# A four-layer model on one core: the pieces of work laid between the steps of an LSTM, cut finer and placed anew

## The reference, cut to what matters

```python
x = x + L0_conv(ln_c(x))   # two Mamba2 blocks along the 32 columns of a row; state and rows in sequence
t = x + L0_ffn(ln_t(x))    # 8 experts of two layers with batch norm, softmax over 8
x = t + L1_conv(ln_c(t))   # log-sum-exp product with an accumulator (V, H, 64, 64)
x = x + L1_ffn(ln_t(x))    # 8 experts, GELU, top 2
x = x + L2_conv(ln_c(x))   # a second log-sum-exp product
x = x + L2_ffn(ln_t(x))    # an LSTM over all 1024 tokens
x = x + L3_conv(ln_c(x))   # 7x7 depthwise convolution, then attention over 1024 tokens
x = x + L3_ffn(ln_t(x))    # 8 experts, top 2

def step(carry, xs):        # of the LSTM, 1024 of them, one after the other
    h, c = carry; xi, xf, xg, xo = xs
    i = sigmoid(xi + h @ V_i); g = tanh(xg + h @ V_c); o = sigmoid(xo + h @ V_o)
    c_new = h * c + i * g
    h_new = o * tanh(c_new)
```

## Time and profile before

| | |
|---|---|
| three runs, median (lowest to highest) | 3486.21 (3484.66 to 3487.12) us |
| the profiled execution, its own time | 3478.68 us |
| its span, first to last instruction | 3476.9 us |
| mean granted TensorE clock | 0.789 |
| first h of the LSTM, last h | 293.7 us, 2842.3 us |
| instructions in the span | 72552 |

### The profile page before, as it was taken

One profiled execution on the slowest core, in us unless ns is written; L12 is line 12 of the kernel. 1 busy time (PEld: TensorE's weight loads), 2 busy tenths in 40 slices (PEclk: granted clock), 3 DMA queues, 4 the chain that ended last, 5 costly groups with the idle time before them and its releaser, 6 DMA issues. The chain is left out here.

```text
span 3476.9 us, 72552 instructions
## 1 busy us (share of the span) xinstructions
PE 2849.0 (82%) x22302; PEld 2325.8 (67%) x22302; DVE 2121.4 (61%) x8884; ACT 1696.4 (49%) x5788; POOL 766.8 (22%) x1419
## 2 busy tenths in 40 slices
PE   4477888898888888889898888889888669887675
PEld 3365666677777777777777777777777554555565
DVE  4566566666666666666666666666644322556777
ACT  1254555555565565555555555555555322443232
POOL 2233222222222222222232222222211000000100
PEclk9687666688787888888888877877867669998677
DMA  2000000000010000000000000000000000000000
GB/s 92 12 16 16 16 17 17 17 18 19 19 31 18 18 18 18 18 18 17 18 17 18 19 19 23 26 18 17 17 16 8 3 16 11 1 1 3 8 7 8
DMA packets 53970, 59.73 MB, mean 17 GB/s; under 512 B 26448, under 2 KB 45008, under 8 KB 53200
## 3 DMA queue, kind: packets, MB, share of 16 engines
q1 hardware_dynamic: 53584, 54.98, 5.3%
HBM read 42.35 MB, written 4.19 MB: 13 GB/s over the span
## 5 line engine op out<-in xcount | busy, mean ns | idle before, releaser
L1116 DVE TENSOR_TENSOR_SCAN r_c<-r_wk 64x24 f32<-64x24 f32 x1024 | 272.6, 266 | 588.8 <-ACT r_wk L1102 576.9
L1091 PEld LDWEIGHTS psL<-r_h,lv 128*64 128x64 f32 x2048 | 244.7, 164 | 509.7 <-DVE r_h L1121 372.8
L1091 PE MATMUL psL<-r_h,lv 128*64 128x8 f32 x2048 | 324.3, 231 | 304.1 <-DVE r_h L1121 271.7
L1102 ACT ACTIVATE r_wk<-psL 64x16 f32<-64x16 f32 x1024 | 189.4, 185 | 688.2 <-PE psL L1092 674.0
L1196 PE MATMUL psL<-img,dg 128*128 (+1 forms) x2744 | 439.9, 318 | 1.1 <-DVE r_h L1121 1.1
L1196 PEld LDWEIGHTS psL<-img,dg 128*128 128x128 f32 x2744 | 399.0, 226 | 6.3 <-issue 1.2
L1107 ACT ACTIVATE r_tc<-r_c 64x8 f32<-64x8 f32 x1024 | 217.2, 212 | 277.0 <-DVE r_c L1116 223.6
L1093 PE MATMUL psL<-r_h,lv 128*64 128x8 f32 x2048 | 330.2, 234 | 0.0
L1092 PE MATMUL psL<-r_h,lv 128*64 128x8 f32 x2048 | 308.2, 223 | 0.0
L1121 DVE SCALAR_TENSOR_TENSOR r_h<-r_wk,r_tc 64x8 f32<-64x8 f32 x1024 | 187.3, 183 | 138.2 <-ACT r_tc L1107 128.9
L1092 PEld LDWEIGHTS psL<-r_h,lv 128*64 128x64 f32 x2048 | 257.7, 174 | 0.0
(11 more groups left out here) (407 smaller groups left out, 6709.0 us busy)
## 6 DMA issues: line engine op xcount, KB each, us to landing
accb<-acc_in SPq DMA_DIRECT2D x64, 512.0 KB, 3.5
a_xy<-a_E SPq DMA_DIRECT2D x512, 16.0 KB, 1.8
W<-pack_in SPq DMA_DIRECT2D x1, 3165.0 KB, 14.1
x6d<-X SPq DMA_DIRECT2D x64, 32.0 KB
out_x<-X SPq DMA_DIRECT2D x32, 64.0 KB, 1.6
X<-x_in SPq DMA_DIRECT2D x1, 1856.0 KB, 18.1
W<-pack_in SPq DMA_DIRECT2D x1, 1331.0 KB, 5.6
X<-x_in SPq DMA_DIRECT2D x1, 192.0 KB, 6.2
```

The lines of the kernel that those rows point to most:

```text
L1091: nc.tensor.matmul(psL[0:64, par, c:c + LB], lv[:, 0], h, start=False, stop=False, skip_group_check=True)
L1102: nc.scalar.activation(o, psL[0:64, par, c:c + 2 * LB].rearrange("p (g b) -> p g b", b=LB), ACT.Tanh).then_inc(sem("r_gi"), 1)
L1116: v.tensor_tensor_scan(r_c3[:, t % 2, :], r_wk[:, 0:24], r_wk[:, 30:54], 0.0, ALU.mult, ALU.add).then_inc(sem("r_c"), 1)
```

## The change

The generators of the parts yield more often, so that a piece is one or two instructions where it was two to eleven, and the rows of `TIMES` have more entries and other due times. `SAME` marks a yield that has no due time of its own where no table is used (in the last phase), so nothing changes there. The hardware loop is gone: all turns are written out by the same Python code. No instruction of the computation is added, removed or altered; only their order on each engine changes, and in the turns of the former loop the waits and addresses are constants in place of register arithmetic.

```diff
 TIMES = {
     mybir.EngineType.SP: (
-        (20.5,), (17.5,), (28,), (11,), (6,),
+        (17,), (13.5,), (28,), (9,), (7.5,),
...
     mybir.EngineType.Activation: (
...
-        (2, 5, 8, 8.5, 10, 13, 20, 25, 30),
+        (3, 3, 5, 5, 8, 8, 8, 9, 10.5, 13, 17.5, 27, 27, 30),
...
@@ mamba_pe
             for j in range(J):
                 if j:
                     yield
                 for h in range(NH):
+                    if h and h % 2 == 0:
+                        yield
                     last = nc.tensor.matmul(...)
@@ mamba_pool
             for j in range(J):
+                if j:
+                    yield
                 last = g.tensor_tensor(u["xw"][:, j], ...)
@@ ffn0_act
                     for q in (2 * n, 2 * n + 1):
+                        if q % 2:
+                            yield
                         last = nc.scalar.activation(f_h[:, q], ..., ACT.Relu, ...)
@@ mix_act
                 for e in (2 * n, 2 * n + 1):
+                    if e % 2:
+                        yield
                     last = nc.scalar.activation(u["h"][:, e], ..., ACT.Gelu, ...)
@@ conv_pe
-                for ky, kx in TAPS[n:n + count]:
+                for c, (ky, kx) in enumerate(TAPS[n:n + count]):
+                    if c and c % 2 == 0:
+                        yield
                     last = nc.tensor.matmul(o, dg[:, ky * KT + kx], rows[...], ...)
@@ weave
                     while due <= slot:
-                        due = next(g, None)
+                        new = next(g, None)
+                        due = due if new == SAME else new
@@ turns
-            with eng.Fori(FIRST_FULL, LAST_FULL, 2) as i:
-                turn(i, FIRST_FULL % 2)
-                turn(i + 1, (FIRST_FULL + 1) % 2)
-            for i in range(LAST_FULL + 1, NT + 1):
+            for i in range(FIRST_FULL, NT + 1):
                 turn(i, i % 2)
```

More of the change, by code:

```diff
@@ L79 @@
     mybir.EngineType.SP: (
-        (20.5,),
-        (17.5,),
+        (17,),
+        (13.5,),
         (28,),
-        (11,),
-        (6,),
+        (9,),
+        (7.5,),
     ),
     mybir.EngineType.Pool: (
-        (29.5, 29.5, 31, 31),
-        (30,),
-        (9.5,),
+        (23.5, 26, 26, 27),
+        (24,),
+        (15,),
         (0,),
-        (10.5,),
-        (11.5,),
-        (0,),
-        (6.5,),
-        (10,),
-        (4, 5.5, 5.5, 21.5),
+        (17, 17.5, 19, 21.5),
+        (22,),
+        (1.5,),
+        (9.5, 11, 14, 14.5),
+        (15,),
+        (5, 5, 8, 8.5, 9, 11.5, 25.5),
         (2.5,),
-        (4, 4.5, 10.5, 22),
+        (6, 6, 6, 6, 14.5, 20, 25),
     ),
@@ L747, in experts_pool @@
             for n in (4, 2, 1):
-                st.did(g.tensor_tensor(big[:, :, 0:n], big[:, :, 0:n], big[:, :, n:2 * n], ALU.add)); st.wait()
+                st.did(g.tensor_tensor(big[:, :, 0:n], big[:, :, 0:n], big[:, :, n:2 * n], ALU.add))
+                yield
+                st.wait()
             st.end()
@@ L813, in prod_dve @@
             pv = ps[0:64, 0, 0:288].rearrange("p (h b t) -> p h b t", h=2, b=B + 1)
-            st.did(v.reciprocal(c_r[k][:], pv[:, :, B])); st.wait()
+            st.did(v.reciprocal(c_r[k][:], pv[:, :, B]))
+            yield
+            st.wait()
             st.end()
@@ L1211, in later @@
             step(*args)
-        END = object()
+        SAME, END = "same", object()
         def weave(parts, tables=None):
```

81 lines of the change are left out of this document (56 added, 25 removed), and 18 rows, old and new, of the table TIMES.

## The result

The changed kernel takes 3215.93 us (median of 4 runs, 3210.49 to 3218.1) against 3485.43 for the kernel before (4 runs, 3481.66 to 3487.12): a ratio of 0.9226, 95% interval 0.921 to 0.9242. I had predicted 3388 with a range of 3300 to 3465: the gain is 270 us where I had 98.5. The direction was right, the size was not.

A forecast was written before the change was run, and what follows sets the result against it. A full turn was taken as a latency chain with a floor plus overfilled pauses, PE idling little, and waits at DMAs and loop jumps. Terms -23.5 - 88 - 12 + 25 = -98.5 us gave 3388 us, range 3300 to 3465.

The forecast's parts named there:

- The loop: Ten jumps back of the hardware loop, where PE waits without a releaser, all go: -23.5 us.
- My end of +20 for fetched code: Unfavourable bound of the loop's removal, if fetching the written-out code costs time: +20 us; 0 was expected.
- The DMA wait: VectorE's waits at the Mamba blocks' additions in turns 1 to 26 go, as copies come earlier and additions later: -88 us.
- The wait moves: Rival, chance 0.2: pieces of steps 24 to 28 become late instead, three quarters of the 88 us return: 3454 us.
- Taps in the last turns: Groups of taps in one pause in turns 28 to 31 are split: 3 us a turn, -12 us.
- The cut pieces in the full turns: Cutting itself buys nothing in turns 0 to 27; PE's wins are lost on ACT: +25 us, ends -60 and +124.
- The sum of overfills: Durations beyond each step's pause, largest of three engines, summed over a full turn: 30.2 us before, 31.8 after.
- The bound of +124: Slow end for the cut pieces' cost in the full turns, taken from the slower rival about ACT: +124 us.
- Table loads: Number of ScalarE table loads is the same in both orders, 62 before the GELUs: 0 us.
- POOL: POOL's work, which lengthens VectorE's chain instructions, is the same but elsewhere: 0 us, bound 120 us either way.
- more than the sum: Rival, chance 0.2: fewer stops keep the mid-turn clock up (58 us), filling turns before the LSTM may give 30: 3300 us.
- The short pause of ACT: Rival, chance 0.1: about twelve ACT pieces between L1104 and L1107 hold back tanh of c; slower, 3530 us.

The follow-up runs named there:

- e11: Changed kernel with the two ScalarE copies that release the Mamba blocks' DMAs laid back at their old, later places: 3311.64 us (0.9536).
- e3: Kernel before with block 0's VectorE addition that waits for DMAs, and the square behind it, laid later: 3481.64 us (1.0017).
- e5: Kernel before with both blocks' VectorE additions that wait for DMAs, and what stands behind them, laid later: 3487.37 us (1.0031).
- e1: Kernel before with its loop removed and all turns written out, nothing else changed: 3439.15 us (0.9903).
- e13: Changed kernel with the convolution's taps alone uncut, each whole group at its first part's new due time: 3398.83 us (0.9785).
- e4: Changed kernel with its new tables but every piece uncut, at the due time of its first part: 3576.31 us (1.0276).
- e6: Changed kernel with an unread VectorE scan before the chain's own in steps 1 to 18 of every turn, 576 in all: 3239.14 us (0.9317).
- e10: Changed kernel without 12 of the convolution's 49 taps, everything else in its place: 3202.94 us (0.9225).
- e18: Changed kernel with the last part of the taps' row spread to due 25, timed together with the changed kernel: 3212.19 us (0.9262).
- e14: Kernel before, written out, with the rows of both Mamba blocks and the mixer cut and laid as in the changed kernel: 3827.19 us (1.0992).
- e7: Changed kernel with an unread VectorE scan before the chain's own in steps 22 to 29 of every turn, 256 in all: 3233.9 us (0.9295).

## Why the prediction was wrong

1. *The loop*, -23.5: mis-sized. It measures -35 in the old order and -49 in the new. The wait was read rightly, but its length isn't its price: in both orders busy time at the low level goes with it, 1.2 to 1.3 us a turn. My end of +20 for fetched code is out. Ahead of the chain's multiplications PE has no wait without a releaser in turns 5 to 26, where the jumps had up to 2.6 us. The weight loads have 197, none over 0.7, which nearly all stand in the same steps of every turn; the kernel before has such ones too, inside its loop, so they are no sign of fetching. By the rule of the Trainium skill ("Runtime: NRT & Kernel Launch", Instruction fetch mechanics: the fetch runs ahead of a straight stream) none was to be expected, and the trace agrees.

2. *The DMA wait*, -88: right in size in the new order, wrong as a separate term. The wait is gone from turns 5 to 26, and e11 prices it at 95. But taken out of the kernel before it is worth 0 (e3, e5). "The wait moves" was the right rival for that edit and the wrong one for this change, which starts the transfers earlier (from step 18, not 21) and lays the tails behind them.

3. *Taps in the last turns*, -12: turns 28 to 31 took 12.7 us less. Right in sum and in its reason: in the mean of these turns steps 1 and 10, which held the most taps in one pause, are 1.6 and 2.1 us shorter, and all others together 0.5 longer. Singly the turns gave 3.9, 2.3, 1.4 and 5.1.

4. *The cut pieces in the full turns*, +25: **this is the step that failed.** Of the 264 us between the spans I take off 2.02 x 22 = 44 for the jumps (e1's trace), 4.4 x 22 = 97 for the idle time of steps 24, 27 and 28 that is gone between e1 and the changed kernel, and 13 for the last turns: 110 are left, where I had +25. It is a remainder and no measured price, as the terms don't add. It holds 8.3 us of DMA waits of turns 1 to 4 and 8.7 us from ahead of the first h, where the sum had no term. The other 93 us have the opposite sign to my term and are nearly four times its size. "So the cutting itself buys nothing" is refuted for the new order by e13 (182 us for the taps' cuts alone) and e4 (360). The sum of overfills took in each step the engine most over its pause and added the steps up: it is blind in three ways. PE's idle time was not in it, 9.2 us a turn, of which 4.8 stood at and behind the additions (steps 24, 27 and 28), 1.1 at the jump and 2.4 in steps 2, 9 and 13, that of step 9 after taps in one lump. A delay of the chain costs little while PE has pieces queued (e6: 0.03 us a turn for a delay of 0.10), so much of what I charged for the ScalarE pieces was probably free; no run moves these alone. And it had no clock: the low level took 28.9 us of a turn before and 20.6 after, since the dips of 3.4 to 6.8 us in mid-turn, around steps 10 and 14 to 16, are gone. The bound of +124 rested on the same accounting.

5. *Table loads*, 0: right, x62 before and after.

6. *POOL*, 0: right as far as the rows show. Where POOL's work strikes the chain is seen in the groups of its two last VectorE lines, before:
```profile
L1121 DVE SCALAR_TENSOR_TENSOR r_h<-r_wk,r_tc 64x8 f32<-64x8 f32 x1024 | 187.3, 183 | 138.2 <-ACT r_tc L1107 128.9
L1123 DVE SCALAR_TENSOR_TENSOR r_wk<-r_h,r_c 64x8 f32<-64x8 f32 x1024 | 198.6, 194 | 35.5
```
and after:
```profile
L1184 DVE SCALAR_TENSOR_TENSOR r_h<-r_wk,r_tc 64x8 f32<-64x8 f32 x1024 | 196.7, 192 | 114.8 <-ACT r_tc L1170 101.3
L1186 DVE SCALAR_TENSOR_TENSOR r_wk<-r_h,r_c 64x8 f32<-64x8 f32 x1024 | 223.4, 218 | 35.5
```
Together 386 and 420 us, more, not less. So it wasn't won here, and by e6 such a delay is mostly hidden behind PE's queued work. By the rule of the Trainium skill ("SBUF — State Buffer", SBUF: two separate sides: one engine has the shared ports for its whole instruction) cutting VectorE's pieces doesn't shorten the lock; the traces agree.

Of the rivals *more than the sum* came nearest, at about half the size of what was missing. Its clock in mid-turn was right. Its filling turns ahead of the first h gave 8.7 us where it had 30, and turns 0 to 4, at which it did not look by themselves, gave 44. *The short pause of ACT* is excluded as what decides here: the kernel is faster, and PE idles 1.4 us a turn. Of my marks, the absent issue waits, the absent waits at the additions and step 24 (1.63 us) came as written. Turns 30 and 31 took 58.5 and 54.7 us, just outside my 55 to 58 on either side. Idle time of 5 to 8 us a turn failed, and it was the sign of the missing gain.

What stays open: why the low stretch at the turn's end keeps a length of 20.5 us in the changed kernel, though PE's records leave only 0.35 us of idle time in the 16.2 us of steps 24 to 31, and how the 110 us of step 4 divide between idle time and clock, as the one comes with the other in every kernel here.

## What to carry to other kernels

Where a latency chain runs between filler pieces on in-order engines, first ask of each step whether the fullest engine has work queued when the chain comes back to it: write a turn as that engine's work, its idle time and what the low clock adds, and price an edit by what it does to these. Don't price rows of such a layout one by one: here the taps' row, exchanged alone, lost 150 us in one direction and 178 in the other, and the whole gained 270. A wait in a profile is worth its length only if what follows it is ready, and that is tested by putting the wait into the better kernel as well as by taking it out of the worse.

## What the runs showed of the hardware

The granted clock changes with the order of work and with its amount. With 12 taps fewer a turn PE had 2.7 us less work and was busy for 4.2 us more at 1.2 GHz (e10). Relaying the same instructions moved the low level's share of a turn between 15.6 of 71.8 us (e18) and 40.7 of 93.6 (e14). Two VectorE scans of 0.20 and 0.17 us, one behind the other, start 0.12 us apart, and the second ends 0.10 us later than it does alone (e7).
